# The written-out instruction orders of all five engines exchanged in a fused attention and expert kernel

## The reference

```python
# 1 tokens: 1024 grid points per image; offsets from a small MLP; 8 sampling points per query
q_feat = bilinear_sample(feature_map, ref)               # 1024 x 64
off = gelu(layer_norm(q_feat @ W_o1 + b_o1)) @ W_o2 + b_o2
sampled = bilinear_sample(feature_map, ref + off*scale)  # 1024 x 8 points x 64: a gather
k, v = sampled @ W_k.T, sampled @ W_v.T                  # attention over the 8 points, 8 heads
# 2 concat with the text (1152 rows), layer norm, causal attention, residual
h = h + softmax(mask(q @ k.T / 8)) @ v
# 3 layer norm, mixture of 16 experts, the 2 best of each row, layer norm, residual
h = h + layernorm(x + sum_k(w_k * expert_k(x))) * gamma + beta
```

## Time and profile before

| what | value |
|---|---|
| median of three runs | 4530.77 us |
| the profiled execution: its own time | 4536.96 us |
| its span | 4534.9 us |
| mean granted TensorE clock | 0.885 |
| PE busy | 3669.2 us (81%) |
| GpSimd (POOL) busy | 3203.0 us (71%) |
| VectorE (DVE) busy | 3077.4 us (68%) |
| ScalarE (ACT) busy | 2199.1 us (48%) |
| DMA | mean 201 GB/s |

### The profile page before, as it was taken

How to read it: one execution, slowest core, us unless ns; L and a number is a source line. 1 busy time by engine, 2 the same in 40 slices (tenths; PEclk the granted TensorE clock), 3 DMA queues, 4 the chain that set the end, 5 groups by cost and what they waited for, 6 DMA issues and landing times.

```text
span 4534.9 us, 82922 instructions
## 1 busy us (share of the span) xinstructions
PE 3669.2 (81%) x26592; PEld 3201.3 (71%) x26592; DVE 3077.4 (68%) x9228; ACT 2199.1 (48%) x5378; POOL 3203.0 (71%) x3089
## 2 busy tenths in 40 slices
PE   4577988888888888888888888888888888877863
PEld 2466877777777777777777777777777777766752
DVE  0485858677695858778595867759586876957331
ACT  2254555455555545554555545455554555544411
POOL 0777677777777777777777777777777777777142
PEclk9888998899989989998999999899899999888755
DMA  8669686776958677686858677685867768542322
GB/s 249 214 188 249 182 262 190 237 215 198 281 142 274 175 238 216 196 256 169 266 165 255 201 226 221 183 268 152 266 183 242 214 200 273 146 143 82 87 71 58
DMA packets 938629, 911.26 MB, mean 201 GB/s; under 512 B 121306, under 2 KB 822362, under 8 KB 938072
## 3 DMA queue, kind: packets, MB, share of 16 engines
q1 hardware_dynamic: 805768, 598.22, 44.1%
q0 software_dynamic: 132432, 307.74, 23.1%
HBM read 583.69 MB, written 323.53 MB: 200 GB/s over the span
## 4 chain that ended last, share of the span: by engine, by line
POOL 30%; PE 27%; issue 12%; DMA 10%; DVE 10%; SPq 6%; ACT 5%; POOLq 0%; DVEq 0%; ACTq 0%
POOL gath L760 14%; POOL xs_d L776 11%; POOL ya L792 5%; DMA fm<-in_x 5%; PE ps L869 3%; PE ps L883 3%; PE ps L814 3%; PE ps L966 3%; PE ps L1034 3%; PE ps L1026 2%; DMA xg<-xs_d 2%; PE ps L944 2%; SPq L705 2%; SPq L674 2%; DMA gath<-table,idx 1%
## 5 line engine op out<-in xcount | busy, mean ns | idle before, releaser
L760 POOL DMA_INDIRECT gath<-table,idx x2048 | 2131.9, 1041 | 790.1 <-issue 649.2
L792 POOL DMA_INDIRECT ya<-ys_d,row x512 | 527.1, 1030 | 355.7 <-DMA ys_d<-yx 189.6
L1234 DVE TENSOR_TENSOR prod<-gath,corner_w 128x1024 f32<-128x1024 f32 x512 | 619.2, 1218 | 214.7 <-DMA gath<-table,idx 194.6
L869 PE MATMUL ps<-const,prod 128*128 128x128 f32 x4096 | 601.9, 295 | 111.1 <-DVE prod L1234 108.9
L883 PE MATMUL ps<-w_kv,samp_t 128*128 128x128 f32 x4096 | 627.5, 302 | 53.3 <-ACT kv_sb L1050 42.3
L776 POOL DMA_INDIRECT xs_d<-xm,row x512 | 534.4, 1044 | 168.2 <-issue 155.2
L883 PEld LDWEIGHTS ps<-w_kv,samp_t 128*128 128x128 f32 x4096 | 571.4, 215 | 81.2 <-issue 62.2
L869 PEld LDWEIGHTS ps<-const,prod 128*128 128x128 f32 x4096 | 520.6, 155 | 145.4 <-DVE prod L1234 120.2
L944 PE MATMUL ps<-k_t,q_t 128*128 128x512 f32 (+3 forms) x960 | 415.8, 525 | 103.8 <-ACT v_sb L1050 67.7
L1234 DVE TENSOR_TENSOR yx<-ps,wx 128x256 f32<-128x256 f32 x320 | 134.1, 419 | 538.6 <-PE ps L1034 538.2
L1050 ACT ACTIVATE rows<-ps 128x512 f32<-128x512 f32 x512 | 304.3, 594 | 356.0 <-PE ps L814 355.1
(11 more groups left out here) (168 smaller groups left out, 6134.9 us busy)
## 6 DMA issues: line engine op xcount, KB each, us to landing
table<-rows SPq DMA_DIRECT2D x224, 1024.0 KB
fm<-in_x SPq DMA_DIRECT2D x256, 512.0 KB
wx<-w_d SPq DMA_DIRECT2D x768, 128.0 KB
gath<-table,idx POOLq DMA_INDIRECT x2048
wx<-w_d SPq DMA_DIRECT2D x64, 512.0 KB
table<-rows SPq DMA_DIRECT2D x32, 960.0 KB
xg<-xs_d SPq DMA_DIRECT2D x192, 130.0 KB
ys_d<-yx SPq DMA_DIRECT2D x192, 128.0 KB
```

What stands on the lines that cost most here:

```text
L760: pool.indirect_dma_start(out=gath[:, n % NG, p, :], out_offset=None, in_=tables[par], in_offset=bass.IndirectOffsetOnAxis(ap=idx[:, par, ...
L792: pool.indirect_dma_start(out=ya[:, k, t, :], out_offset=None, in_=ys_d[par], in_offset=bass.IndirectOffsetOnAxis(ap=row[:, par, n:n + 1], ...
L869: last = pe.matmul(bank(0, p * P, p * P + P), prod[h][:, (p * 2 + dx) * P:(p * 2 + dx + 1) * P], ident, is_transpose=True, start=(dx == 0) ...
L1234: return dve.tensor_tensor(o, a, b, op)
```

## The change

All strings of `TURNS` and `LAST` are exchanged: those of TensorE, ScalarE, VectorE, GpSimd and SyncE. Each string has the same letters as before in the same numbers; no stage, instruction, buffer or semaphore changes. The change calls itself: all engines' strings remade by a random walk over a replay in which GpSimd's transfers wait for VectorE's long two-operand products.

```diff
 TURNS = {
     "tensor":
-        "xxtxtkxtkxgtgakgatxgaaaxgagxssxtkgqxsatxgsqxsgkgxqtxgkgsxgagxagxtxsgsqgxkgtxgaxgkgxqsxgqsxtqkxtagsqa"
+        "xxtxtkgtxkgtakgxatgaaxagxaxstsxgqkxsgqtgaxsgxkxqagxtgxkgsgsxagqsgxtsxgaxkgxtxqgkxqgxtsgxsgkqgtxgqaxg"
...
     "gpsimd":
-        "pppppppffffffffffffffffpppffffffffffffffffccccccccccccccccccccccccccccccccpppppp",
+        "pppppppffffffffffffffffpfpfffffpffcfffccffcccfccccfcccfccccccccpcccccccccccppppp",
     "sync":
-        "ggxxgxxgxgxxxggxgxgxxhxgxxxgggggggggggxxgehgxgxxxexxxxxx",
+        "ggxxxggxxxgxggxxxggxxxxxgghxggxgggxggggggxeggxxxhxexxxxx",
```

More of the change, by code:

```diff
@@ L244 @@
     "tensor":
-        "xxtxtkxtkxgtgakgatxgaaaxgagxssxtkgqxsatxgsqxsgkgxqtxgkgsxgagxagxtxsgsqgxkgtxgaxgkgxqsxgqsxtqkxtagsqa"
-        "xtxkgsagqtgkgaqtgssqagsqakqgaaqaqagagkggtgaagkagkgagtgkggtgkgtgkgtgrgkgtgxgkgtgxkgxagaxgaaatasxsksqs"
-        "axqtsaxqksxaqsgtxsqasgqxkaastqsxsqktkxaxaqxkxqsaqxssqatxaqkqtqxakaxaatxtxkxktaxkaaxaxx",
+        "xxtxtkgtxkgtakgxatgaaxagxaxstsxgqkxsgqtgaxsgxkxqagxtgxkgsgsxagqsgxtsxgaxkgxtxqgkxqgxtsgxsgkqgtxgqaxg"
+        "sgatxkgqksgagtgaqsqstqsagakqagaqaqaagkggtgagkgaakgagtgkggtgkgtgkgtgrgkgtgxkgxgtxgkxagagagaaastkqsasx"
@@ L248 @@
+        "sqtxasxksqxaqxsgasxtqgsqskxkatastqxkaqsxqakxqssasxqatqxakqxtqaxkxqaaaxttxkxkataxkaaxxx",
     "scalar":
-        "xxttkxtagkgatxgaaaaagtaxgagvkxstqsxgkxgtsgvqgxqkgxggstgxgkxgtgsxqvgxkgsggxqtxkqtqkgxtvxsqggktggqtsqg"
-        "vkqggqskqgqqggtggaagvkaagkagatvgkggtgkggtgkgtvgaktgggkgtgxgkvagxagagatagakxaaeeeavstsqxgqskqtssqxgqv"
-        "kqkxtsqstkexqtkeeqxsvqqqxstkvqqktqvxxtkxtkxaavktaakaaxvxa",
+        "xxttkgtxakgatagaxaagtaxagaxskqtgvsxgskgxqgxtgxkggqsgvkxgtqxggxtskxgqgtxkvgxtqgsggqvxgtqgkxsgtkgqggst"
@@ L252 @@
+        "qqgvkqsgkqqqggtggaagvakgakgaagtkvgtggkggtkgtgvagtkgggkgxtgvxgkagaaaggaagaaxtkateseeqvssqkxqgsxqsvgtq"
+        "kqstxktkqsvxteeqekqsqxqktqvsxkqtxqqvxkttxkaxakatvaaakxvxa",
     "vector":
-        "wawaaxawwaaaaaaaaaaawvvxwwvvaaxvvwaavvvvvvxavavxaavwaawaavxvvvavawxwavvvaxaavvvwwvvavvvvaxvvvvaawaav"
-        "waaavvvavavvaawaaaaaaaaaaaaaaaavwvvvvvvveveeeaaavaeeeeaaawwavvavvveaeveeeevaaaraavvevvwaewrvraraeara"
-        "rvavvaaaaaaaraavevrrrrvvrxrwwvrgggggggggggvgeeegxggggggeeeeegggwevaxvgaexvvexaaagvaggxxaevaaaxxavavv"
@@ L256 @@
-        "vwxaxxaavaevvvxavxeeeeeeeggeeeaeeewxaeevevgeeeaeeeveexgxaagxxageexxexgxxgavxavwaaxvavvvxvvawvvvvvvva"
-        "vxxawvxvvavwaxaaaaaaaawaaaaaavvvvvvxvvvvvvvvaaaaaaaaxaaaavvaaa",
+        "wawaaaaawaaaxaawaaaavwxwvvvaaxwawvvaavxvavvavvaxawawvaavvxvvavavvwxwavvvvvvvxvaaawwvavxaavvavwwvaaav"
+        "avvavavvawvaavvaaaaaaaaaaaaaavaawvvvevvveevevaeaaaeaavevvavavwwveavevaaavaeeevraawvavvwvrearrrvaraar"
+        "aaaeaearrvaaeeerreaaarevxvrvrvvvwwgeggggeveggeggggggegggggegggaggwvxexeaeaxvxavaavaxvvxxvexeaeagexva"
@@ L258 @@
+        "veaegeeaxegvewxexaveaaexegevegvgwgeaeeeexgavvvegvxgeaeeeagxwaxaxavavvxaaaexvxvxaaevxvvwvvxvaxxvvvxax"
+        "vvxawwavaavxaaaavaaaaaaaaavwvvvvevvvxvvvvaavaaavavaaxaaaavaava",
     "gpsimd":
-        "pppppppffffffffffffffffpppffffffffffffffffccccccccccccccccccccccccccccccccpppppp",
+        "pppppppffffffffffffffffpfpfffffpffcfffccffcccfccccfcccfccccccccpcccccccccccppppp",
     "sync":
-        "ggxxgxxgxgxxxggxgxgxxhxgxxxgggggggggggxxgehgxgxxxexxxxxx",
+        "ggxxxggxxxgxggxxxggxxxxxgghxggxgggxggggggxeggxxxhxexxxxx",
@@ L264 @@
     "tensor":
[L265 to L268, removed]
+        "xxtxtxktktaxatxaaxakasxssqxaxstktxkqtxqxasxkxsxtxaqtxksxaxskxqxsqxsktxqaxktxasxaqqtsqtsaktssqaaqaqak"
@@ L269 @@
+        "qakqaataakakaktkttkktrtxkxxktaxataaaksaxssqstqaxsaxksqasqxsxaskqtsxqaqxsattksqxkaxqassxqqakxxsqatxax"
+        "qqkatqakxaatxtxkxtkaxakaxaxxxxxxxaaxaaxaaxssxsqxsxaqxxaqxsxqxasxsxxsxaxqxxsqxqsxaxxsqaasqaqsqssaqaqa"
+        "qaqaaaaaaarxxxxxxxxxxxxxxxxxxxxxxxxxxxxxxxxxxxxxxxxxxxxxxxxxxxxx",
     "scalar":
-        "xxttkxtakatxaaaaataxavkxstqsxkxtsvqxqkxstxkxtsxqvxksxqtxkqtqkxtvxsqktqtsqvkqqskqqqtaavkaakaatvktktkt"
-        "vaktktxkvaxaaataakxaaeeeavstsqxqskqtssqxqvkqkxtsqstkexqtkeeqxsvqqqxstkvqqktqvxxtkxtkxaavktaakaaxvxax"
@@ L272 @@
-        "xxaaxaaaaaaxaxsqsxxsqxqxsxxsxqxsxqxqqxxsqqsqqqsqqqaaaaaaaxxxeeexxxexeexxxxxxxxxxxxxxxxxxxxxxxxxxeeee"
+        "xxttkxtakatxaaaaaxvatkasxsqtsxkxtvqxtqkxsxtsxqkxkvxsqxqktxtkxtqvxsqqtktskvqqsqqkqqktavaakakaatvkttkk"
+        "tvaktvtkxxtaaaakaaxeaaeeastvqsskqxsqktqxvstqkqsxsqttkxeeqevsqqxkqqxsktvqqktqxvtkxxtkxaavtkaaakaxxvxa"
+        "xxaaaxaaaaxaaxsqxssxqsxxqxxqxxssqxxqqxxsqqqsqsqqqqaaaaaaaxxeeexxxxeexxexxxxxxxxxxxxxxxxxxxxxxxxxeeee"
         "ee",
     "vector":
-        "wawaaxawwaaaaaaaaaaawvvxwwvvaaxvvwaavvvvvvxavavxaavwaawaavxvvvavawxwavvvaxaavvvwwvvavvvvaxvvvvaawaav"
@@ L276 @@
[L276 to L280, removed]
@@ L281 @@
-        "xxeexxexxxxxxxxxxxxxxxxxxxxxeeeeeeeeeeeeeeeeeeeeeeeeeeeeeeeeeeeeeeeeeeeeeeeeeeeeeeeeee",
+        "waawaxaaawaaaaaaaawawvxvvwwvaaxvvavaavwwvvvvxaavavvxvwaaavvvaxvavawxwvaavvvavwvxvawvaxvaavvvvawvwava"
+        "aavvaaaavvavwvaaaaaaaaaavaaaaaavwvvvvveevevveevaavveawaeaeawvevavaeeaeaavavrveaveavawvvaraerraveeaea"
+        "vraavervaaaaaerrrwvraaawvvxerwerrvreexeexvevwveaavxeaaavavxvaxavvaxavaxxxvevvaeaxwaeeaevxeeeaeexevxa"
+        "eavwxeaeeevexeexeeeeeeeaxavavxeaeavexxxvavaxvxxwaxvavvxavwvvvvvavaxvvwvxaavwaxaaaaaxaawaavaaavvavvvv"
@@ L282 @@
+        "vxvvvvvvaaaaaaavxaaaavavaavaaaaaaxaaaaaaaaaaxaxaaaaaxaxaaaxaaaaaxxaaaxaaaaaaaaaaaaaaaaaaaaaaaaaaaaae"
+        "eeaeaeeaeaaaaaaeeeeeeaaaraarrraeererrerrxrrerrerxxeeeeeeexeeeeexexeeexexeeexxeeeeeeeeexeexexxexexexx"
+        "exxxxxxxxxxxexxxxxxexxexxxxxeeeeeeeeeeeeeeeeeeeeeeeeeeeeeeeeeeeeeeeeeeeeeeeeeeeeeeeeee",
     "gpsimd":
-        "pppppppffffffffffffffffpppffffffffffffffffccccccccccccccccccccccccccccccccppffffffffffffffffffffffff"
-        "ffffffffccccccccccccccccccccccccccccccccffffffffffffffffffffffffffffffff",
+        "pppppppffffffffffffffffpfffpfffffpccccfffccfcccffffcccccccccccccccccccccccppffffffffffffffffffffffff"
@@ L285 @@
+        "fffffffccfccccccccccccccccccccccccccccccffffffffffffffffffffffffffffffff",
     "sync":
-        "xxxxxxxxxxxxhxxxxxxehxxxxexxxxxxxxxxxxxxxxxxxxxxxxexxxxexxxxxxxxxxxxxxxxxxxxxxee",
+        "xxxxxhxxxxxxxxxxxhxxexxxxxxxxxxxxexxxxxxxxxxxxxxxxxexxxxxxxxxxxxxxxxxxxxxxxxexee",
 }
```

## The result

The changed kernel takes 4672.77 us (median of four runs, 4655.6 to 4676.15), the kernel before 4532.86 us beside it. The ratio is 1.0289, 95% interval 1.0264 to 1.0314: slower, by 140 us. The forecast was 4502 us with a range up to 4562. The profiled execution after took 4655.6 us, its span is 4653.6 us and the mean granted clock 0.861 (0.885 before).

What follows compares the result with a forecast made beforehand. GpSimd's full transfer stream was taken as the bound. Fewer collisions (19 us) and a shorter wait at the 41st transfer (10 us) gave 29 us, everything else 0: 4530.8 - 29 = 4502 us, range 4460 to 4562.

Steps and rivals of the forecast that it cites:

- What bounds the kernel: GpSimd's stream of 192 transfers a period is full, 258 of 260 us, and its period is the kernel's.
- a second limit near: At GpSimd's 41st transfer: its buffer waits for product 12, behind TensorE's expert group 17; 2.25 us stood where 0.30 is normal.
- Collisions, -19 us: GpSimd transfers held by VectorE products: three more products directly behind two-operand instructions save 1.35 us a period, 19 us.
- the phase of the others: All other VectorE products meet GpSimd's transfer beat anew: by 3 us a period either way, +-40 us over 14 periods.
- rival A: Nothing gained, 4531 us: new collisions cost what the old did, or savings are waited out at the 41st transfer; chance 0.26.
- The wait at the 41st transfer, -10 us: Loads of groups 11 and 13 go ahead of tables 0 and 1, taking 10 of 23 us from GpSimd's wait.
- The fetches, costed at 0: Last fetch 17.6 us later, VectorE waits at least 5.9 us at the second combine, hidden by seam gather waits; uncovered 84 us.
- The scatters, costed at 0 "by a hair": Scatters end 8 transfers, 10.8 us, later, and group 8's load with them; 3 us left for landing, cost 0.
- Rival B: Late scatters delay group 8's load, then product 12 and the 41st transfer, if landing exceeds 3 us: about 4560 us, chance 0.24.
- as it said for being right: Signs: mean transfer 1033 ns, gather issue 518 us, period 258 us, second combine waiting 6 us or more, shorter seam waits.
- its mark for being wrong: The forecast is wrong if GpSimd's mean transfer in the steady periods, 1040 ns, doesn't move or rises.
- rival B's two: Signs: waits of several us at the 41st or 81st transfer every period, with TensorE waiting for `xg` or `wx` at group 8.

Runs made afterwards that it cites:

- e6c: The kernel before with only SyncE's changed strings: 4526.4 us, ratio 0.9986.
- e5: The kernel before with GpSimd's last eight fetches mixed among the scatters, last fetch 125th transfer instead of 112th: 4618.54 us, ratio 1.0194.
- e4c: The kernel before with the last eleven scatters behind one more round of gathers, last scatter 152nd instead of 144th: 4550.45 us, ratio 1.0029.
- f2: The kernel before with the last eleven scatters of a period behind two more rounds of gathers: 4648.82 us, ratio 1.0271.
- e1: The changed kernel with GpSimd's strings of before, the other four engines' strings new: 4615.64 us, ratio 1.0186.
- e10c: The changed kernel with the orders of before for GpSimd and for SyncE's turns: 4687.64 us, ratio 1.0337.
- f1: e1 with the gathers of products 29 to 32 ahead of the last eleven scatters: 4739.75 us, ratio 1.0458.
- f5: e1 with VectorE's products 29, 30 and 31 moved 10, 3 and 9 stages later; only on the slow chips: ratio 1.059, earlier runs 1.0647 and 1.0583.
- e2: The kernel before with GpSimd's new strings alone: 4629.35 us, ratio 1.0212.

## Why the prediction was wrong

*What bounds the kernel* was right for the kernel before: GpSimd's stream, 258 of 260 us, with a second limit near. In the change GpSimd stands 11 us a period in waits beyond the usual issue, so there the way through VectorE and TensorE sets the period.

*Collisions, -19 us.* Not found. The mean of all transfers went from 1040 to 1042 ns. Summed over a period, what transfers take beyond 945 ns went from 18.3 to 18.7 us, where a fall by 1.35 was counted; that lies well within the +-3 us given for the phase of the others. This part of rival A held.

*The wait at the 41st transfer, -10 us.* SyncE's order alone takes some 17 us of this waiting away (e6c), and the median fell by 9 us; but in its trace longer transfers took nearly all of it back, so the nearness of 9 to 10 is no proof of the term. In the change the later products overran it.

*The fetches, costed at 0: this is the step that failed.* The prediction saw the wait and sized it: 5.9 us plus the landing, some 9 us, and e5 measured 9.1. It took VectorE's waits for gathers for its cover, and for the case without it gave 6 us x 14 = 84 us. e5 costs 88 us. That the two agree is partly luck: the 84 leave out the landing, and the uncovered wait would be 9.1 x 14 = 127 us. The cover was spent, all 8.1 us of it, but it was VectorE's. TensorE stands behind the same combine (`att_m`), is busy 85% of a period, and gave back 1.9 us of 8.5; product 12 stands behind `yx`, which comes from TensorE. So the delay went round VectorE's reserve and reached the 41st transfer.

The way can be added up, as means of nine periods. Before: from the start of the 41st transfer to the end of the last fetch 96.5 us, from there 11.3 us to the second combine, which waited for nothing, then 151.8 us to the end of product 12 and 1.0 us to the next 41st transfer. In e5 the same four are 113.7, 5.3, 147.5 and 0.8, together the period of 267.3; in the change 119.2, 4.3, 147.0 and 0.8, together 271.1. Behind the combine the way shrank by 4.3 us in e5, not by the 8.1 us of the cover. The loop is closed, with a wait at each of its handoffs, and so it sets the period. That the cover was on the wrong engine is read from these traces; that the late fetches cost it is shown by e5.

*The scatters, costed at 0 "by a hair".* Close: e4c gives 15 us. Rival B's mechanism is real, and f2 shows it at 118 us, but in the change it doesn't act: there, group 8 keeps its 14.3 us from load to use, because TensorE is late as well. B named the right trigger point: the prediction left 3 us for the landing, which took 2.2, so that 14.0 - 2.2 - 10.8 = 1.0 us remained.

*Left out altogether:* the orders of VectorE, TensorE and ScalarE. The prediction looked at them for collisions and for single neighbours, and never asked how the work between two handoffs had shifted. With GpSimd's old order they cost 85 us (e1), SyncE's part of it being none (e6c, e10c). Shown is where it surfaces: the way from product 29 to product 15 of the next period is 7.9 us longer, all of it behind product 12 and all of it VectorE standing, and the period 7.1 us. That this way sets e1's period is argued, not shown: f1 put another delay in its place, and f5 ran only on the other chips. Which engine's order makes the attention tiles late was not tried either.

The parts alone are 88 (fetches), 15 (scatters) and 85 us (other engines), 188 in all, and the change costs 140: by the readings above they lie on loops that share the stretch from the combine to the 41st transfer; no run shows how they share it. e2, all of GpSimd's new order, costs 98, which e5's 88 can't be told from; group 8 keeps 13.4 us from load to use in it, so the late scatters have no visible part there. No chance had been given to a loss above some 32 us (4563), though the prediction had written the 84 us down. Its signs came mixed: the second combine waited over 6 us and the waits for gathers at the seam went, as it said for being right; the mean transfer didn't fall, its mark for being wrong; and of rival B's two, waits of several us stood at the 41st transfer in every period, but not with TensorE waiting at group 8.

## What to carry to other kernels

A wait counts as cover only for the engines that stand in it: before costing a new wait at nothing, list everyone queued behind the waiting instruction, and look for reserve on each of them, above all on the engine that is 85% busy. Where two engines hand to each other twice a period, sum the way between the handoffs as a loop, old order against new; orders can hold the same work and differ by 8 us there. Margins are kinks: read from the trace how far a load's issue lies ahead of its use (14.0 us) and take off its landing (2.2 us). Here a shift of 10.8 us, just inside the rest, cost 15 us, and one of 21.6 us cost 118.

## What the hardware showed unexpectedly

The kernel before took 4520 to 4546 us on some chips and 6706 to 6936 us on others. In e6c's kernel, profiled on one of the latter, VectorE's 512 products take 1218 ns each as on an ordinary chip, and GpSimd goes on with its transfers at 1.25 us each while ScalarE stands up to 30.5 us for no recorded reason. VectorE has such waits too, and TensorE stands with them. In several stretches of over 20 us none of the three had an instruction. What holds them there, the traces don't say. An order tuned on one kind of chip need not be the better one on the other: the late scatters of e4c are 0.3% slower on the one and 0.3% faster on the other, with intervals of about 0.1 and 0.2%.
